# A four-layer graph network on one core: coefficients of the fourth loop spread by DMA, and more columns gathered by TensorE

## The reference, cut to what matters

```python
h = jnp.maximum(_layernorm(x), 0.0)
x = x + mean over edges (h[src] * edge_attr_32) + h          # layer 0
x = x + softmax attention of Q[dst], K[src], V[src], then Wo  # layer 1, plus h
x = x + segment_sum(h[src], dst) @ W                          # layer 2
# layer 3: 9 coefficients per edge (1 + 3 + 5) couple with the 32 features of h[src]
#   msg = sum over c of  coef[e, c] * (h[src] @ T_c),   T_c a 32 x 32 matrix
x = x + segment_sum(msg, dst)
return x
```

## Time and profile before

| | us |
|---|---|
| median of three executions | 13893.11 |
| the profiled execution, device time | 13869.06 |
| its span, first to last instruction | 13867.2 |
| POOL busy | 11498.1 |
| VectorE (DVE) busy | 11170.5 |
| TensorE (PE) busy | 11075.0 |
| ScalarE (ACT) busy | 3293.7 |

### The profile page before, as it was taken

One profiled execution on the slowest core, in us unless ns is written; L12 is line 12 of the kernel. 1 busy time (PEld: TensorE's weight loads), 2 busy tenths in 40 slices (PEclk: granted clock), 3 DMA queues, 4 the chain that ended last, 5 costly groups with the idle time before them and its releaser, 6 DMA issues.

```text
span 13867.2 us, 198598 instructions
## 1 busy us (share of the span) xinstructions
PE 11075.0 (80%) x49235; PEld 8972.2 (65%) x49235; DVE 11170.5 (81%) x15127; ACT 3293.7 (24%) x3628; POOL 11498.1 (83%) x19996
## 2 busy tenths in 40 slices
PE   7999999991666666666569999899859999999995
PEld 6888888881545554554458888888836666666663
DVE  8988989984999999999877777777757777777775
ACT  2222222220333333333222222222201111111110
POOL 6888888887888888888778888888878888888887
PEclk9999999995777777777789999999979999999997
DMA  3323333331232322223222222222222222222221
GB/s 106 86 82 94 94 94 91 81 86 37 73 84 71 83 76 81 77 77 80 57 65 66 67 70 70 71 68 67 62 45 50 57 50 55 52 55 53 55 53 34
DMA packets 863909, 963.05 MB, mean 69 GB/s; under 512 B 426441, under 2 KB 678253, under 8 KB 863105
## 3 DMA queue, kind: packets, MB, share of 16 engines
q1 hardware_dynamic: 396088, 456.93, 12.1%
q0 software_dynamic: 327744, 170.03, 8.6%
q10 hardware_dynamic: 139400, 330.44, 6.2%
HBM read 614.57 MB, written 341.90 MB: 69 GB/s over the span
## 4 chain that ended last, share of the span: by engine, by line
issue 48%; POOL 47%; DVE 2%; POOLq 1%; PE 1%; DMA 0%; ACT 0%; SPq 0%; DVEq 0%; ACTq 0%
POOL rows L418 33%; POOL work L423 11%; POOL outs L432 2%; POOLq L422 1%; POOL q_edges L397 1%; PE psum L554 0%; PE psum L631 0%; DVE work L935 0%; DVE work L937 0%; POOLq L416 0%; PE psum L592 0%; DVE rows L767 0%; DVE h_parts L710 0%; DMA idx<-src_c 0%; DVE work L703 0%
## 5 line engine op out<-in xcount | busy, mean ns | idle before, releaser
L418 POOL DMA_INDIRECT rows<-h_table,idx x9750 | 9651.2, 990 | 2093.0 <-POOL work L423 1701.5
L554 PE MATMUL psum<-h_parts,one_hot 128*128 128x448 f32 x38808 | 8674.5, 384 | 681.4 <-ACT one_hot L461 669.9
L554 PEld LDWEIGHTS psum<-h_parts,one_hot 128*128 128x128 f32 x38808 | 7609.7, 198 | 1582.1 <-issue 790.1
L461 ACT ACTIVATE one_hot<-bit_hot 128x896 fp32r<-128x896 bf16 x2177 | 2057.8, 951 | 6984.1 <-DVE bit_hot L740 6943.8
L761 DVE TENSOR_TENSOR tile_rows<-psum,h_mask 128x448 f32<-128x448 f32 x2772 | 1721.1, 621 | 925.5 <-PE psum L554 720.9
L631 PE MATMUL psum<-work,bd_t 128*128 128x512 f32 (+1 forms) x4500 | 1766.9, 521 | 191.6 <-DVE work L1133 110.8
L767 DVE TENSOR_REDUCE rows<-tile_rows 128x32 f32<-128x448 f32 x2772 | 1694.0, 611 | 0.0
L631 PEld LDWEIGHTS psum<-work,bd_t 128*128 128x128 f32 x4500 | 823.2, 196 | 915.0 <-issue 596.9
L423 POOL MEMSET work<- 128x32 f32 x9750 | 1404.0, 144 | 3.6
L1118 DVE TENSOR_TENSOR work<-psum,work 128x800 f32<-128x800 f32 x1125 | 1102.7, 989 | 318.5 <-PE psum L622 250.0
L740 DVE TENSOR_TENSOR bit_hot<-keys,target 128x896 bf16<-128x896 int16 x2177 | 1343.6, 617 | 11.0 <-issue 11.0
(11 more groups left out here) (176 smaller groups left out, 6020.9 us busy)
## 6 DMA issues: line engine op xcount, KB each, us to landing
rows<-h_table,idx POOLq DMA_INDIRECT x9750
sums<-outs ACTq DMA_DIRECT2D x375, 400.0 KB, 2.4
dwin<-keep_rows SPq DMA_DIRECT2D x1500, 100.0 KB
attn<-outs ACTq DMA_DIRECT2D x125, 800.0 KB, 3.4
dwin<-dst_w SPq DMA_DIRECT2D x500, 100.1 KB
edge_in<-pattern_c SPq DMA_DIRECT2D x125, 400.0 KB
q_edges<-work ACTq DMA_DIRECT2D x25, 2000.0 KB
edge_in<-q_edges SPq DMA_DIRECT2D x125, 400.0 KB
```

Of the source, the lines that this page charges most:

```text
L418: nc.gpsimd.indirect_dma_start(out=rows[:, r, j * D:(j + 1) * D], out_offset=None, in_=h_table[:, :], in_offset=bass.IndirectOffsetOnAxis( ...
L461: nc.scalar.activation(one_hots[i % TILE_BUFS[l]][:, :, :], bit_hots[i % BIT_BUFS[l]], ACT.Copy).then_inc(one_hot_cast, 1)
L554: last = nc.tensor.matmul(banks[TILE_BANKS[l][b]][:, 0:H0 * D], one_hots[b][:, h1, :], h_parts[:, part, h1 * H0 * D:(h1 + 1) * H0 * D], st ...
```

## The change

- `PE_COLS` becomes 7.2 (as before), 6, 8 and 4.8 columns: 17.8, 19, 17 and 20.2 gathers per chunk stay on POOL. The fourth loop has four tile buffers instead of two, the third loop two bit buffers instead of three.
- Fourth loop: `spread` is gone. `sh_c` is laid out as one row of 800 values per chunk, group and coefficient, and ScalarE's queue loads each row onto 32 partitions in fp32 (`load_coefs`): 16 DMAs per chunk in four parts (coefficients 0 to 1, 2 to 4, 5 to 6, 7 to 8), 4 groups each, single-buffered in `edge_in` and in the second halves of `outs`. A part of the next chunk is loaded when its coefficients were weighed in this one. `hT` moves to PSUM (`in_ps`), and `weigh` multiplies the coefficients in SBUF by it.
- Third loop: the split into bf16 parts, its load and its store are gone.
- Running sums `O` and, in the second loop, `mz` move to PSUM in the first three loops, so the transposes into `outs` read PSUM there. The second loop's six picks per chunk stand two behind L994, two behind L1004 and two behind the last transpose. The constant `sel` and its load and copy are gone.

```diff
-PE_COLS = ((7, 7, 7, 7, 8), (4,) * RING, (7, 7, 7, 7, 8), (4, 3, 4, 3, 4))
+PE_COLS = ((7, 7, 7, 7, 8), (6,) * RING, (8,) * RING, (5, 5, 5, 4, 5))
-BIT_BUFS = (3, 2, 3, 2)
-TILE_BUFS = (3, 2, 4, 2)
-TILE_BANKS = ((4, 5, 7), (4, 5), (2, 3, 4, 5), (4, 5))
+BIT_BUFS = (3, 2, 2, 2)
+TILE_BUFS = (3, 2, 4, 4)
+TILE_BANKS = ((4, 5, 7), (4, 5), (2, 3, 4, 5), (2, 3, 4, 5))
+COEF_PARTS = ((0, 2), (2, 5), (5, 7), (7, 9))
...
+        coefs = [edge_in[:, n, :] for n in range(RING)] + [outs[:, n, CH:2 * CH] for n in range(SH - RING)]
...
-                        if l == 2:
-                            sp.wait_ge(edge_used[r], t + (2 * TURNS + START))
-                            sp.dma_start(edge_in[:, r, 0:J * SH], sh_c[c].rearrange("o p c -> (o p) c")).then_inc(edge_loaded[r], 16)
-                        if l == 3:
-                            sp.wait_ge(bcast_ready, t * (RING * SH) + (r * SH + START))
-                            sp.dma_start(shT[r], sh_split[c].rearrange("o k (g e) -> (o k g) e", e=CH)).then_inc(shT_loaded[r], 16)
...
+                if l == 3:
+                    for loaded in coef_loaded:
+                        pool.wait_ge(loaded, (NCH + 1) * 16 * G)
...
-                    cast_next(1, t, r, range(2, PE_MAX))
+                    cast_next(1, t, r, range(2, 4))
                     store(1, t, r, attn_chunks, 2 * CH)
+                    cast_next(1, t, r, range(4, PE_MAX))
...
+            def load_coefs(t, r, k):
+                a, b = COEF_PARTS[k]
+                c = bass.ds(r if t is None else t * RING + r, 1)
+                for g in range(G):
+                    to = edge_in[D * g:D * g + D, a:b, :] if b <= RING else outs[D * g:D * g + D, a - RING:b - RING, CH:2 * CH]
+                    act.dma_start(to, sh_c[c, g, a:b, :].broadcast_to([D, b - a, CH])).then_inc(coef_loaded[k], 16)
+            def load_next_coefs(t, r, k):
+                act.wait_ge(weighted_ready, t * (RING * SH) + (r * SH + COEF_PARTS[k][1] + START))
+                load_coefs(t, r + 1, k)
...
             cast_first(3)
             with act.Fori(0, TURNS) as t:
                 for r in range(RING):
-                    cast_next(3, t, r, range(PE_MAX))
+                    load_next_coefs(t, r, 0)
+                    cast_next(3, t, r, range(2))
+                    load_next_coefs(t, r, 1)
+                    cast_next(3, t, r, range(2, 3))
+                    load_next_coefs(t, r, 2)
+                    cast_next(3, t, r, range(3, 4))
+                    load_next_coefs(t, r, 3)
+                    cast_next(3, t, r, range(4, PE_MAX))
                     store(3, t, r, sums_chunks, CH)
...
-                    spread(t, r, 0)
-                    spread(t, r, 1)
                     gather_tile(3, t, ahead[0], per_turn[3])
                     for n in range(SH):
                         couple(t, r, n)
-                        if n + 2 < SH:
-                            spread(t, r, n + 2)
                         if n % 2 and n // 2 + 1 < len(ahead):
                             gather_tile(3, t, ahead[n // 2 + 1], per_turn[3])
...
-                    pick_next(1, t, r, range(2, PE_MAX))
+                    pick_next(1, t, r, range(2, 4))
...
-                    then(nc.vector.tensor_tensor_scan(O, u, in_ps, last_of(O), ALU.mult, ALU.add))
+                    then(nc.vector.tensor_tensor_scan(in_ps, u, in_ps, o_last, ALU.mult, ALU.add))
                     v.wait_ge(mz_m_ready, n)
-                    then(nc.vector.tensor_copy(mx[:, 0:1], mx[:, CH:CH + 1]))
-                    nc.vector.scalar_tensor_tensor(out=mz, in0=Z, scalar=half[:, 1:2], in1=acc_wide, op0=ALU.mult, op1=ALU.add)\
-                        .then_inc(mz_ready, 1)
-                    v.wait_ge(mz_ready, chunk_no(0, t, r, START))
+                    nc.vector.tensor_copy(mx[:, 0:1], mx[:, CH:CH + 1])
+                    nc.vector.tensor_copy(o_last, last_of(in_ps))
+                    then(nc.vector.scalar_tensor_tensor(out=acc_wide, in0=Z, scalar=half[:, 1:2], in1=acc_wide,
+                                                        op0=ALU.mult, op1=ALU.add))
                     v.wait_ge(outs_stored[r], t * 16 + (1 * TURNS * 16 + START))
                     row = outs[:, r, :].rearrange("p (j f) -> p j f", j=J)
-                    then(nc.vector.transpose(row[:, :, 0:D], by_edge(O)))
-                    nc.vector.transpose(row[:, :, D:2 * D], by_edge(mz)).then_inc(outs_ready[r], 1)
+                    nc.vector.transpose(row[:, :, D:2 * D], by_edge(acc_wide)).then_inc(mz_ready, 1)
+                    nc.vector.transpose(row[:, :, 0:D], by_edge(in_ps)).then_inc(outs_ready[r], 1)
+                    v.wait_ge(mz_ready, chunk_no(0, t, r, START))
+                    v.wait_ge(outs_ready[r], use(1, t))
+                    pick_next(1, t, r, range(4, PE_MAX))
...
-                    v.wait_ge(edge_loaded[r], use(2, t) * 16)
-                    v.wait_ge(sh_stored, t * (16 * RING) + (16 * r + START))
-                    sh_f = edge_in[:, r, 0:J * SH]
-                    then(nc.vector.tensor_copy(sh_parts[:, 0, :], sh_f))
...
                 at = r * SH + n
-                v.wait_ge(bcast_ready, t * (RING * SH) + (at + 1 + SPREAD_START))
+                k = [a <= n < b for a, b in COEF_PARTS].index(True)
+                v.wait_ge(coef_loaded[k], t * (RING * 16 * G) + (r + 1) * 16 * G)
                 v.wait_ge(weighted_used, t * (RING * SH) + (at + START))
-                nc.vector.tensor_tensor(weighted[n % 3], bcast[n % 2], hT, ALU.mult).then_inc(weighted_ready, 1)
+                nc.vector.tensor_tensor(weighted[n % 3], coefs[n], in_ps, ALU.mult).then_inc(weighted_ready, 1)
...
                         pick(3, t, ahead[n // 2 - 1])
                     weigh(t, r, n)
+                for i in ahead[SH // 2:]:
+                    pick(3, t, i)
```

More of the change, by code:

```diff
@@ L162, in gnn_kernel @@
         half = sb("half", [P, 3])
-        sel = sb("sel", [P, SH, P], BF16)
         staged = [0]
@@ L524, in _ @@
                 std(3 * PIECES + q)
+            def load_coefs(t, r, k):
[7 more added lines that the diff above has]
+                load_coefs(t, r + 1, k)
+            for r in range(RING):
+                act.wait_ge(edge_used[r], 2 * TURNS + START)
+            act.wait_ge(parts_ready, PIECES * LAYERS)
+            for k in range(len(COEF_PARTS)):
+                load_coefs(None, 0, k)
             cast_first(3)
@@ L614, in _ @@
                 mix(2 * PIECES + q, bd_w2)
-            def spread(t, r, n):
-                pe.wait_ge(weighted_ready, t * (RING * SH) + (r * SH + max(n - 1, 0) + START))
-                if n == 0:
-                    pe.wait_ge(shT_loaded[r], t * 16 + 16)
-                for cols in SPANS:
-                    last = nc.tensor.matmul(bcast[n % 2][:, cols], sel[0:SH_ROWS, n, :], shT[r][:, cols], start=True, stop=True)
-                last.then_inc(bcast_ready, 1)
             def couple(t, r, n):
@@ L1109, in next_rows @@
                 v.wait_ge(picked, tile_no(tile_base, 3, t, first_tile(3, r + 2)))
-                nc.vector.transpose(by_edge(hT), rows[:, r1, :]).then_inc(rows_used[r1], 1)
+                nc.vector.transpose(by_edge(in_ps), rows[:, r1, :]).then_inc(rows_used[r1], 1)
                 v.wait_ge(rows_used[r1], use(3, t, START + more))
@@ L1144, in _ @@
             v.wait_ge(picked, tile_no(tile_base, 3, 0, first_tile(3, 1)))
-            nc.vector.transpose(by_edge(hT), rows[:, 0, :]).then_inc(rows_used[0], 1)
+            nc.vector.transpose(by_edge(in_ps), rows[:, 0, :]).then_inc(rows_used[0], 1)
             v.wait_ge(rows_used[0], use(3, 0, START))
@@ L1222, in constants @@
     inner = np.where(feature < mul, feature, (feature - mul) // 3)
-    sel = np.zeros((P, SH, P), np.float32)
-    row = np.arange(SH_ROWS)
-    for c in range(SH):
-        sel[0:SH_ROWS, c, :] = (row[:, None] // SH % G == group[None]) & (row % SH == c)[:, None]
     cg = coupling_coefficients()
```

59 lines of the change are left out of this document (21 added, 38 removed).

## The result

The changed kernel takes 13970.61 us (median of 5 runs, 13942.52 to 13983.4) against 13893.11 of the kernel before: a ratio of 1.0056, with a 95% interval of 1.0041 to 1.0070. That is slower by 77 us. The forecast was 13920, with a range of 13750 to 14110, and "slower" was its likeliest case. The profiled execution took 13970.94 us, against 13869.06 before, so the two traces lie 102 us apart.

What follows compares the result with a forecast made beforehand. The prediction took POOL's gathers to set the pace in all four loops. Second loop +131, third -79, fourth -25 and first 0 sum to +27 us on a 13893 median: 13920, range 13750 to 14110, the forecast's own 13860 to 13980.

Steps and rivals of the forecast that it cites:

- Second loop, forecast +131: Second loop at six columns: VectorE becomes the bound, 28.4 us per chunk against 27.35, +131 us, bounds +80 and +310.
- 28.0 us: Second loop: VectorE's instructions in a row per chunk, 25.86 + 3.38 for picks + 0.15 for a copy - 1.37 for transposes.
- I keep 0.4: Second loop: VectorE's wait for tiles at a pick, 0.6 us per chunk before, taken as 0.4 after.
- Third loop, forecast -79: Third loop at 8 columns: 23.3 us per chunk against 23.93, -79 us, bounds -105 and 0.
- TensorE: 8 x 2.9 = 23.2, now the bound: Third loop: eight tiles of 2.9 us each make TensorE the bound at 23.2 us per chunk, POOL at 22.9.
- Fourth loop, forecast -25: Fourth loop at 4.8 columns: 27.6 us per chunk against 27.82, -25 us, bounds -190 and +60.
- The walk along both queues: Fourth loop, chunk's end: from the last tile's end X, next `couple` 0 starts at X + 6.1, TensorE standing 1.8 us.
- 130.4 + 7.2: Fourth loop, TensorE's turn of five chunks: 130.4 us of tiles and couples plus 4 stands of 1.8 us.
- First loop, forecast 0: First loop: columns stay, scan and transpose through PSUM stand on VectorE, which is not the pace: 0 us.
- POOL's pace in the fourth loop: Rival, chance 0.22: fourth loop's stand at the chunk's end is covered, 26.3 us per chunk, -190 us, total 13755 us.
- Slow reads from PSUM: Rival, chance 0.15: strided PSUM reads leave the second loop's two transposes slow, +171 us more, total 14091 us.
- The coefficients come late or crowd the gathers: Rival, chance 0.08: coefficient loads cost the fourth loop 2 us per chunk, adding 250 us, about 14170 us.

Runs made afterwards that it cites:

- experiment 1: The changed kernel with the second loop back to four columns, the rest of the change kept: 13927.17 us (8 runs), ratio 1.0015 to the kernel before.
- experiment 2: The changed kernel with the first loop's running sums back in SBUF: 13967.83 us (5 runs), ratio 1.0049 to the kernel before.
- Experiment 3: The changed kernel with the fourth loop's tiles after each even `couple` instead of each odd one: 13933.02 us (7 runs), ratio 1.0031 to the kernel before.
- experiment 4: The changed kernel with coefficients loaded only for the first chunk and used for all chunks: 13952.32 us, one run.
- experiments 3 and 4 together: The changed kernel with fourth-loop tiles after each even `couple` and coefficients loaded only once: 22376.06 and 22387.95 us, one run each, on the slow chips.
- shifted: The changed kernel with four second-loop columns and 120 fulfilled waits ahead of VectorE's fourth loop: 22059.63 and 22069.69 us on slow chips, ratios 1.0059 and 1.0065.

## Why the prediction was right

The sign was right, and the time lies within the range and even within the forecast's own 13860 to 13980. The size is less good: the sum was +27 us, the traces differ by 102 and the medians by 77. The second loop came out 38 us, the fourth 28 and the first 39 above their terms, the third 32 below. That the total stayed inside the narrow range is partly luck, as told below at the branch. Step by step:

**Second loop, forecast +131, measured +169.** "28.0 us" for VectorE's instructions in a row is right: the window less its waits is (3520 - 52.0 - 18.9)/122.6 = 28.13. The transposes from PSUM, the unknown of the sum, stand as groups of the page's kind (busy, mean ns, idle before), with the copy of a column:

```profile
L1019 DVE STREAM_TRANSPOSE outs<-psum 128x800 f32<-128x800 f32 x125 | 127.1, 1017 | 6.7
L1020 DVE STREAM_TRANSPOSE outs<-psum 128x800 f32<-128x800 f32 x125 | 121.7, 973 | 0.0
L1014 DVE COPY o_last<-psum 128x1 f32<-128x1 f32 x125 | 18.5, 148 | 0.0
```

They take 1.99 us together against the forecast's 2.06 and 3.42 before. Two other terms of the row missed and cancelled: from start to start in the trace the two picks are 3.6 us, not 3.38, and the second copy cost nothing, since both copies now take 0.14 us from start to start where the one took 0.19. The rows' transpose gave 0.1 of that back (median 1789 ns, 1674 before). The term for late tiles, "I keep 0.4", was 0.15 (18.9/122.6): TensorE's mean granted clock is 0.91 with six tiles per chunk to make, where it was 0.77 with four (0.77 with four again in experiment 1). What was missed is the branch, which has no term in the sum: 52.0 us in 24 waits, 0.42 per chunk. It had no row in this loop before. 28.13 + 0.42 + 0.15 = 28.70. Over 125 chunks the branch is +53, the longer row +16 and the fewer late tiles -31, from 131 to 169.

**Third loop, forecast -79, measured -111.** "TensorE: 8 x 2.9 = 23.2, now the bound" is right in kind: it is busy for 2827.93 of 2830 us. A tile takes 14 x 0.2055 = 2.88 us (2828/13764 each), and the 0.1 us kept for disturbance was not needed: 23.03. The four buffers of tiles cover VectorE entirely. POOL is level with it, as "two engines within 0.3 us of each other" says: it never stands there but at the branch, and from about 8650 us on VectorE waits for its rows (window 7320 to 10150 us).

```profile
DVE psum L1081 <- DMA rows<-h_table,idx: 66.4, 46, 3.1
POOL rows L405 <- issue: 60.2, 24, 3.5
```

**Fourth loop, forecast -25, measured +3.** The walk along both queues holds to a tenth of a microsecond. One chunk's end in the timeline of the kernel after:

```profile
11012.41 1.51 PE L635 MATMUL psum<-work,bd_t 128*128 128x512 f32 x4
11012.61 0.62 DVE L761 TENSOR_TENSOR tile_rows<-psum,h_mask 128x448 f32<-128x448 f32 x1 [2.91 <-PE psum L567]
...
11013.53 3.26 PE L567 MATMUL psum<-h_parts,one_hot 128*128 128x448 f32 x14
...
11014.43 1.03 DVE L1103 STREAM_TRANSPOSE psum<-rows 128x800 f32<-128x800 f32 x1
11015.65 0.99 DVE L1112 TENSOR_TENSOR work<-edge_in,psum 128x800 f32<-128x800 f32 x1 [0.19 <-DVE psum L1103]
11016.55 1.87 DVE L1129 TENSOR_TENSOR_SCAN work<-dwin,work,psum 128x800 f32<-128x800 f32 x1
11018.48 2.95 PE L635 MATMUL psum<-work,bd_t 128*128 128x512 f32 x8 [1.69 <-DVE work L1129]
```

From X = 11012.41, `couple` 0 starts at X + 6.07 (forecast X + 6.1) after a stand of 1.69 us (forecast 1.8). The waits give 164.1 us in 97 times, four chunks of five. A turn's five chunks take 29.18, 28.73, 24.21, 28.6 and 28.56 us, 139.3, where the forecast's 130.4 + 7.2 and a little more gave 138. The waits for `weigh` are 22.8 us in 24 turns, 0.9 per turn, and the first chunk of a turn is 0.5 us longer than its like; the remainder of about a microsecond per turn I cannot place.

**First loop, forecast 0, measured +39.** "Both stand on VectorE, which is not the pace" is right about the scan and the transpose (experiment 2: 0.08 us), but the loop still lost 0.31 us per chunk on POOL, as gathers and branch.

**What the forecast did not know it owed.** VectorE's stand of 3.14 us at the fourth loop's branch was there before (80.7 us in the 23 waits of L749), hidden behind POOL. By experiment 1 it would have cost 28.70 - 27.84 = 0.86 us per chunk (106 us) once the loop had become TensorE's and VectorE's. The change took it away by chance, and put one worth 53 us into the second loop. Had it stayed, the same traces would give some 200 us over the kernel before, still in the range of 13750 to 14110 but outside the forecast's own.

**The rivals.** *POOL's pace in the fourth loop* did not come: the stand is there. Experiment 3 shows that taking most of it away gives 27.57 and not 26.3, since POOL's own turn then holds 8.5 us of branch. *Slow reads from PSUM* is refuted by L1019 and L1020. The Trainium skill (SBUF — State Buffer, "Door 1: The DMA port swizzle") says that non-contiguous access in PSUM slows matmuls; carried over to VectorE's transposes with a stride of 100 bytes, that does not hold here (1.02 and 0.97 us). *The coefficients come late or crowd the gathers* is refuted for this kernel: no `weigh` waits for one, and without their loads a chunk is 0.2 us shorter (experiment 4), not 2. Where POOL is the bound, as in experiment 3, the loads do cost through the branch. The DMA share was 0.82, not the 0.71 of the forecast (19.5 of 27.6), so the rate taken for them was too high, but the slack covered it.

**What stays open.** Whether four columns in the second loop with the fourth loop's code where it is after the change beats the kernel before. By rows, experiment 1's 13836.6 us less 0.86 x 124 would be 13730, or about 13810 with the third loop at 23.03; the kernel before has a span of 13867.2. This is an estimate: its only runs were on the slow chips, where it is 0.6% slower than the kernel before. Nor was it settled there what 4.8 columns in the second loop, four in the fourth, or experiments 3 and 4 together are worth where POOL or VectorE is the bound. How the loads lengthen POOL's stand is open as well.

## What to carry to other kernels

Before work is moved off the engine that sets the pace, add up every other engine's instructions per chunk from the trace, waits taken out: that sum was right to 0.5% here, and it said that two columns too many went to an engine with 1.5 us to spare. Where an accumulator is single, follow both queues past the last step of a chunk and ask what stands there, as the price was found to a tenth of a microsecond; and when the stand is taken out, expect the old bound close behind it. Look for waits "for issue" that come once per turn of a loop, before and after: editing one loop can move such a stand into or out of another whose code is the same.

## What the runs showed of the hardware

- **The branch at a loop's end** took 0.2 to 0.3 us or 2.4 to 3.3 us (medians). On VectorE it went with where the code lies: 3.02 against 0.23 us for one loop body, moved by the 60 instructions that the 120 waits became (the two traces are from different chips). On POOL it was also long in some turns while the coefficients were loaded: 7.8 to 9.4 us at every branch of experiment 3's fourth loop, 7.9 to 9.7 at the first four of the kernel after, but in the fourth loop never over 3.6 at the usual speed without the loads (experiment 4 and the kernel before). That the fetch of code is what takes the time, and waits behind those loads, is my reading and was not shown.
- **The pitch of TensorE's matmuls**, from start to start, differed between streams without a gap at full granted clock. The tile matmuls (128x448) of the third loop in the kernel after and in experiment 1, both over the whole window:

```profile
L567 PE MATMUL psum<-h_parts,one_hot 128*128 128x448 f32 x13764 | 2828.4, 367 | 2.1 <-ACT one_hot L451 2.0
```

```profile
L567 PE MATMUL psum<-h_parts,one_hot 128*128 128x448 f32 x13702 | 2740.6, 362 | 0.0
```

  These are 205.5 and 200.0 ns each, 23.03 and 22.40 us per chunk with the same code. Experiments 2 and 4 have 206.7 and 206.6 in that loop. What sets the pitch stays open; of the five traces at the usual speed with eight tiles, the one at 200.0 is also the one where POOL stands 0.21 us at the branch. Experiment 1's eight runs lie apart too (13836.7 to 13886.02 in three, 13925.95 to 13935.83 in five), and 0.63 us over 124 chunks would be 78 us of that, but only one of them was traced.
- **Gathers** took 0.95 us (median) and up to 1.98 beside VectorE's comparisons of two operands in SBUF.
- **Transposes of 128x800** in float32 took 0.97 to 1.07 us (means and medians by line) where the strided side was in PSUM, read or written, and 1.67 to 1.79 where it was in SBUF.
- **Chips differ**: two took 1.58 times as long for the kernel before (21936 and 21930 us against 13893), at a mean granted clock of 0.75 against 0.90, with gaps between TensorE's matmuls that have no releaser in the trace. The kernel with four columns in the second loop, level with the one before on the first chip (unshifted), was 0.6% behind it there (shifted).
